# A mask bias and a table of root steps, placed earlier in GpSimd's order

## The reference

```python
x = x + xattn0(layernorm(x), ctx, ctx, mask, Wq, Wk, Wv, Wo)   # 16 heads of 64, per batch of 512
x = x + ffn0(layernorm(x), ...)                                # 8 experts, each takes its top tokens
x = x + xattn1(layernorm(x), ctx, ctx, ...)                    # 16 heads of 16, band of 128
x = x + ffn1(layernorm(x), ...)                                # groups of experts per token
# xattn0: energy = Q K^T / 8;  energy = where(mask == 0, -1e20, energy);  softmax(energy) V;  @ Wo
```

## Time and profile before

| what | value |
| --- | --- |
| runs | 1150.3, 1155.9, 1155.79 us |
| profiled execution | 1150.3 us, its span from first to last instruction 1148.5 us |
| TensorE busy | 1045.3 us, 91% of the span |
| VectorE, ScalarE, GpSimd busy | 750.4, 672.5, 556.1 us |
| TensorE's granted clock, mean | 0.966 |
| first attention | to about 500 us |

### The profile page before, as it was taken

The page is one execution under the profiler, slowest core; times in us unless marked ns, Lnnn a source line. Parts: engine busy times, 40 slices in busy tenths (PEclk is TensorE's granted clock), DMA queues, the critical chain, the costliest instruction groups (busy, mean ns, idle before and its releaser), DMA issues. The chain is left out here.

```text
span 1148.5 us, 28788 instructions
## 1 busy us (share of the span) xinstructions
PE 1045.3 (91%) x10247; PEld 767.7 (67%) x10248; DVE 750.4 (65%) x2151; ACT 672.5 (59%) x1273; POOL 556.1 (48%) x685
## 2 busy tenths in 40 slices
PE   6999999999999999975699997799989857999995
PEld 3666777777777777764488884355454446888885
DVE  5887887788878877968411125677777774555552
ACT  6887876787768867856422235376766643334331
POOL 4677644666556653301447630776666522233312
PEclk9999999999999999995899999899999978999998
DMA  7633333333344334309546546324344221111200
GB/s 259 169 79 93 84 75 79 88 85 75 66 93 93 76 75 93 75 11 343 174 129 187 178 101 217 110 85 139 121 125 147 84 96 34 30 33 26 32 11 10
DMA packets 124380, 117.22 MB, mean 102 GB/s; under 512 B 47840, under 2 KB 104416, under 8 KB 124128
## 3 DMA queue, kind: packets, MB, share of 16 engines
q1 hardware_dynamic: 116960, 106.32, 32.9%
q0 software_dynamic: 7296, 9.25, 4.8%
HBM read 59.89 MB, written 21.82 MB: 71 GB/s over the span
## 5 line engine op out<-in xcount | busy, mean ns | idle before, releaser
L810 DVE TENSOR_TENSOR e_t_lo<-et,e_t_hi 128x512 f16<-128x512 f32 x256 | 176.6, 690 | 45.7 <-ACT e_t_hi L697 43.7
L704 ACT ACTIVATE e<-masked,neg_max 128x512 f32<-128x512 f32 x256 | 184.4, 720 | 37.7 <-DVE neg_max L836 34.9
L836 DVE CUSTOM_DVE_ANT_0 masked<-sc,mask_bias 128x512 f32<-128x512 f32 x256 | 175.4, 686 | 30.7 <-issue 26.2
L697 ACT ACTIVATE e_t_hi<-et 128x512 f16<-128x512 f32 x256 | 151.6, 592 | 71.1 <-PE et L581 69.7
L581 PEld LDWEIGHTS et<-ident,e 128*128 128x128 f32 x1024 | 124.5, 140 | 56.7 <-issue 8.7
L581 PE MATMUL et<-ident,e 128*128 128x128 f32 x1024 | 154.4, 273 | 1.0 <-ACT e L704 0.8
L2260 ACT ACTIVATE d_e<-d_st 128x384 f32<-128x384 f32 (+1 forms) x192 | 93.9, 526 | 50.2 <-PE d_st L2403 45.8
L74 PE MATMUL ob<-v_hi,e_t_hi 128*128 128x65 f16 x1024 | 119.0, 193 | 1.2 <-issue 1.2
L75 PE MATMUL ob<-v_lo,e_t_hi 128*128 128x65 f16 x1024 | 119.2, 193 | 0.0
L76 PE MATMUL ob<-v_hi,e_t_lo 128*128 128x65 f16 x1024 | 118.4, 193 | 0.0
L74 PE MATMUL h_hb<-h_xt_hi,experts_hi 128*128 128x256 f16 x352 | 96.8, 275 | 3.8 <-DVE h_xt_lo L2634 3.8
(11 more groups left out here) (496 smaller groups left out, 2741.6 us busy)
## 6 DMA issues: line engine op xcount, KB each, us to landing
kk<-nat_k SPq DMA_DIRECT2D x64, 256.0 KB, 3.5
raw<-in_fc SPq DMA_DIRECT2D x16, 1024.0 KB, 7.6
qq<-nat_q SPq DMA_DIRECT2D x64, 128.0 KB, 2.6
qk<-scratch_stack SPq DMA_DIRECT2D x64, 128.0 KB
scratch_stack<-kq_hi SPq DMA_DIRECT2D x16, 256.0 KB, 3.0
scratch_stack<-kq_lo SPq DMA_DIRECT2D x16, 256.0 KB, 3.2
d_expert_raw<-in_gate_w SPq DMA_DIRECT2D x8, 512.0 KB, 3.6
d_expert_raw<-in_up_w SPq DMA_DIRECT2D x8, 512.0 KB, 3.8
```

The lines of the kernel that those rows point to most:

```text
L697: nc.scalar.activation(e_t[u % NBUF].hi[:], et[u % 2][:], ACT.Copy).then_inc(turned_hi, 1)
L704: nc.scalar.activation(e[u % NBUF][:], masked[u % NBUF][:], ACT.Exp, bias=neg_max[:, g % 2, j:j + 1], scale=-1.0).then_inc(exp_ok, 1)
L810: nc.vector.tensor_tensor(e_t[u % NBUF].lo[:], et[u % 2][:], e_t[u % NBUF].hi[:], ALU.subtract).then_inc(turned_lo, 1)
L836: nc.vector.tensor_tensor_reduce(masked[u % NBUF][:], sc[j % 2][:], mask_bias[g // PAIRS % 2][:, j % QT, :], -SCALE0, 3e38, ALU.add, ALU.m ...
```

## The change

Two conditions. The 14 steps of kind "z" stand at pair 3, j = 6 in place of pair 4, j = 3; `bias` of the tiles 0 to 3 of the next batch stands in pairs 3 to 6 in place of 4 to 7, at j = 2 as before. The steps of kind "r" stay. `load_mask` in SP's loop is not touched: it stands in pairs 3 to 6.

```diff
@@ newton_of
-    if (p, j) == (4, 3) and b + 1 in LATE_OF["z"]:
+    if (p, j) == (3, 6) and b + 1 in LATE_OF["z"]:
         return "z", b + 1
@@ GpSimd's loop
-                        if j == 2 and g // PAIRS + 1 < B and 0 <= g % PAIRS - MASK_PAIR - 1 < QT:
-                            bias((g // PAIRS + 1) * QT + g % PAIRS - MASK_PAIR - 1)
+                        if j == 2 and g // PAIRS + 1 < B and 0 <= g % PAIRS - MASK_PAIR < QT:
+                            bias((g // PAIRS + 1) * QT + g % PAIRS - MASK_PAIR)
```

## The result

The changed kernel takes 1164.58 us, the kernel before 1155.31 us (medians of 7 runs each; 1158.87 to 1169.02 and 1150.3 to 1156.08). The ratio is 1.0088, 95% interval 1.0062 to 1.0114: slower by 0.9%. The prediction said 1159.9 us, a range of 1153.5 to 1164.5, and "within 0.5%" as likeliest. The time is just above the range, and the kernel is slower by more than 0.5%. The waits that were forecast for batch 0 came; the cost of 0 for batches 1 and 2 did not hold.

A forecast was written before the change was run, and what follows sets the result against it. The prediction took TensorE's own work to bound the first attention, GpSimd costing only where it makes something late. Batch 0's 2.8 + 0.7 + 0.6 = 4.1 us, batches 1 and 2 nothing, on 1155.79 gave 1159.9 us, range 1153.5 to 1164.5.

The forecast's parts named there:

- gap of TensorE for `qq`, first score of pair 5: Batch 0: the 14 steps delay the k and q splits, so TensorE waits for qq, 2.8 us with nothing over it.
- `normalize`, pair 5: Batch 0, pair 4's normalize: waits 2.4 us for the o split, less 0.92 covered; 0.7 us more than before.
- `normalize`, pair 6: Batch 0, pair 5's normalize: waits 1.55 us for the o split, less 0.92 covered; costs 0.6 us.
- `normalize`, pair 7: Batch 0, pair 6's normalize: waits 0.65 us for the o split, wholly covered; costs nothing.
- cover of 0.92 us: First attention: 0.92 us of a VectorE wait lies under the units TensorE is ahead; used for every such wait.
- Batches 1 and 2 ... Cost 0: First attention, batches 1 and 2: qq in time, normalize waits 0.1 us, covered, next pairs within 0.2 us; cost 0.
- The prediction's own sign of being wrong: Also wrong if pair 5 of batch 0 starts on time or stages after 500 us move by more than the shift.
- forecast of 3.2 us from a mask's issue to its bias: GpSimd's bias, pairs 3 to 6: each waits for its mask, landed 3.2 us after SP issues the load.
- The 0.5 us that the prediction put behind the last packet: Mask loads: an estimated 0.5 us for the semaphore between a mask's last packet and its landing.
- Rival C: First attention: masks land 1.5 us later, about 4.7 us from issue; +18 us in all, 1174 us; chance 0.11.
- B: First attention: masks arrive before GpSimd needs them, qq before 93.47, only the removed wait counts; -0.75 us, 1155.0; chance 0.12.
- D: TensorE's clock falls to 1.2 GHz in the new gap, costing 2.8 us; +6.9 us, 1162.7 us; chance 0.07.

The follow-up runs named there:

- e0: The kernel before, unchanged, run and traced once more: 1155.02 against 1155.42 us, ratio 0.9991, first attention 447.63 us.
- e1: The kernel before with only the 14 steps of kind "z" moved earlier, the bias not: ratio to before 0.9986, attention 446.56 us.
- e4: The changed kernel, unedited, run and traced once more: 1161.41 against 1152.92 us, ratio to before 1.0083, attention 456.39 us.
- e8: The changed kernel with the small VectorE steps of kind "r" three units earlier: ratio to the kernel before 1.0052, attention 456.19 us.
- e9: The kernel before with the small VectorE steps of kind "r" three units later: attention 448.55 us, one run.
- after: The first profiled execution of the changed kernel, against the kernel before: 1166.58 us, attention 456.76 us.
- e2: The kernel before with only the bias a pair earlier, the 14 steps not moved: ratio to before 1.0124, attention 460.68 us.
- e5: The changed kernel with masks loaded ahead of the stacking on SP in pairs 3 and 4 only: attention 449.89 us, one run.
- e6: The changed kernel with masks loaded ahead of the stacking on SP in pairs 5 and 6 only: attention 451.02 us, one run.
- e10: The changed kernel with SP's four transposes of the routed part one pair later: attention 460.94 us, one run.
- e3: The changed kernel with all mask loads ahead of the stacking on SP: 1155.83 us, ratio to before 1.0005, attention 447.05 us.
- e7: The kernel before with the bias a pair earlier but at j = 6, behind the o split: ratio to before 1.0016, attention 447.46 us.

## Why the prediction was wrong

**Batch 0: right in mechanism, in its sum partly by luck.** Against e0, pair by pair:

| step | predicted | measured |
| --- | --- | --- |
| gap of TensorE for `qq`, first score of pair 5 | wait 2.8, cost 2.8 | wait 2.50, pair 4 +2.67 |
| `normalize`, pair 5 | waits 2.4, +0.7 | waits 2.21, +0.57 |
| `normalize`, pair 6 | waits 1.55, +0.6 | waits 1.25, +0.62 |
| `normalize`, pair 7 | waits 0.65, 0 | waits 0.67, +0.39 |
| sum | 4.1 | 4.25 |

The four waits are there and within 0.3 us. The costs agree less well than their sum: two are 0.13 us smaller, the last is 0.39 instead of nothing. The 0.62 of pair 6 for a shorter wait is no hit either: without a wait that pair takes 14.21 us (e1), not the 14.58 of e0, so the wait cost 0.99 and only 0.26 were covered. And in e4, the same kernel, batch 0 lost 6.1 us. One sum of the prediction is off by 0.1 us: 77.80 + 0.5 is 78.3 and not 78.2, which would make the wait for `qq` 2.9.

**The cover of 0.92 us was the first wrong term.** It came from one place, pair 5 of batch 0, and there it holds: without a wait the pair takes 14.19 us (e1), after 15.48 with a wait of 2.21, so 0.92 were covered. Elsewhere it doesn't. Pair length over that without a wait, against the wait: (1,5) 1.37 for 1.65, (1,6) 1.07 for 1.06, (2,5) 0.42 for 0.70, (0,7) 0.40 for 0.67. That is a cover of 0 to 0.3 us. In e4 it is 0.6 in (0,6), 2.21 for 2.81, against the 14.21 us of e1: it is no constant of a pair either. One reading of the trace of before could have warned of it: pair 5 of batch 1 is busier on VectorE than that of batch 0 (12.66 of 14.18 against 10.63 of 14.93 us in the earlier trace rows). e8 speaks for it: with the steps of kind "r" earlier VectorE is busy 12.22 us in (1,5) and (2,5) instead of 12.46, and there 0.54 us were covered in both (1.28 for 1.82, 0.05 for 0.59). That is one execution, and the edit was not made to test this.

**The step that failed is "Batches 1 and 2 ... Cost 0".** It measured 3.5 and 1.4 us, and 1.5 and 1.6 in e4. The prediction's own sign of being wrong, batches 1 and 2 longer by over 1 us each, came in both executions. The margin there was 0.1 us of wait plus the cover. Three things went over it:
- A mask that landed late. The mask of pair 4 was issued at 217.62 and its bias started at 222.75, 5.1 us later, where the prediction had 3.2; `normalize` at 228.34 waited 1.65 instead of 0.1, and the next one 1.06: +1.37 and +1.08 us. In e4 the same mask took 3.87 us, `normalize` waited 0.26, (1,5) had no loss and (1,6) +0.43. There mask 6 of batch 0 took 4.69 us instead, and (0,6) lost 1.84.
- The two small VectorE steps in pair 7, some 0.8 and 0.5 us, of which the prediction had nothing (experiments e8, e9). It asked who waits for GpSimd's splits, not who runs beside them.
- The queue of SP in batch 2, whose place ahead of the stacking I didn't read. The prediction said that "the next two pairs come out within 0.2 us likewise" for batch 1 and took batch 2 as the same. (2,5) lost 0.43 us, and (2,6) 0.23.

**The landing time.** The forecast of 3.2 us from a mask's issue to its bias was the usual case. Over the seven profiled executions with such waits (after, e4, e8, e2, e5, e6, e10) there are 73 of them. The page has two queues for instructions, q8 and q14. In 56 of the waits no packet of q8 moved in between, and they took 2.67 to 3.66 us. In the other 17 one did: 3.00 to 5.42, and all nine above 3.7 are among these. No run tells whether the packets are the cause. Rival C, 1.5 us later each time, put its cost at +14 over the forecast; in the four executions with all 12 masks behind the splits and the steps moved (after, e4, e8, e10) one to three masks in 12 took more than 3.7 us, and that is what the range should have carried. The 0.5 us that the prediction put behind the last packet was right: in after and e4 the bias started 0.3 to 0.6 us behind the last packet of any DMA in 23 of 24 cases. Its ground for it was not: a whole qq of 2.7 us leaves room for 2 us behind the last byte.

**Rivals.** B is refuted: all masks are waited for. C is true of single masks only. D, the fall of the clock in the new gap, got 0.07. In the profiled execution it did not happen, in the second one it did. A stretch of e4, columns as above:

```profile
97.00:100.00 3.00, 3.00 (x22) 1.93 (x21) 1.38 (x4) 1.69 (x3) 1.78 (x1) 0.50 0.15 53
```

The same of the changed kernel's first execution:

```profile
98.00:101.00 3.00, 3.00 (x35) 2.08 (x34) 1.78 (x6) 1.69 (x3) 2.03 (x2) 1.00 0.12 43
```

Both are the 3 us behind the gap, of 2.41 and 2.50 us. At 0.50, the level of 1.2 GHz, TensorE starts 22 matmuls, at 2.4 GHz 35. Its price is smaller than D's 2.8 us: from the first to the second score product of the pair 4.19 us against 2.54, +1.65. And it is not simply added. With it (0,5) takes 15.85 us and `normalize` waits only 0.59, under the cover, since it comes later itself; without it 15.48 and 2.21. So D changes what the losses are called and adds 0.4 us here.

**What was right**: 12 waits of the bias; pairs 3 and 4 of batches 1 and 2 unchanged; the k and q splits as the critical ones behind the 14 steps; the worth of the steps alone, 0.74 us; the later phases moved by no more than executions of the same kernel differ.

**The median.** The forecast, 4.1 us, was put on 1155.79. The measured attention makes 9.1, so 1155.31 + 9.1 = 1164.4, against 1164.58 measured. Nothing of the size is left over that the scatter would let one see.

Left open: what makes a mask land late; what makes one execution some 6 us longer after 500 us; and whether a second buffer for o would take the waits off VectorE. That last was not tried.

## What to carry to other kernels

Before an instruction is moved ahead of a transfer's arrival, look where that transfer is issued. Here the masks stood on SP behind the very splits that GpSimd now held up by waiting for them; with the load moved too (e3) the same change costs nothing that was measured. A cover measured at one wait holds for that place alone: take it anew for every stage, and give an in-order queue with 0.1 us to spare the latest landing that the trace shows, not the median. And ask of each moved instruction what it will run beside, not only who waits for it.

## What the runs showed of the hardware

- A VectorE step of 0.16 us took 0.66 to 1.02 us beside a two-input fp32 to fp16 operation of GpSimd of 1.12 to 1.16 us, and ended 0.02 to 0.03 us behind it. Beside a one-input int32 to bf16 operation of 1.94 us it took 0.57 and ended before it (e7).
- TensorE's clock, from full, in the first attention: behind gaps of 3.32, 3.54 and 3.73 us it fell to 1.2 GHz each time, behind gaps of 2.41 to 2.52 us in three executions of five (e4, e6 and e8 yes; after and e10 no), behind gaps of 1.00 to 1.92 us in none of four. A fall cost 1.65 to 1.67 us where it can be read against the changed kernel's first execution (e4, e6, e8, from the first to the third score product of pair 5). The case of e10, TensorE's granted clock 0.53 over the stretch:

```profile
365.00:368.50 3.50, 3.50 (x23) 2.05 (x22) 1.38 (x4) 1.21 (x2) 2.82 (x3) 0.53 0.03 7
```

The Trainium skill ("TensorE: Matmul & The Clock Gate", section "Part 1: The HAM clock gate (the "warmup" mystery)") says of the slow stretch at a kernel's start that it varies from run to run. Here it is the fall behind a gap that varies, over five gaps of nearly one length.
- A 256 KB load of a mask from HBM took 2.7 to 3.7 us from its issue to the start of its reader in 64 of 73 cases, 3.9 to 5.4 in the other nine.
